# Attention rows normed one step later: inverses turned, moved and applied at later steps, three gate fills and one key projection moved with them

## The reference, cut to what matters

```python
a1 = _attn(q, k1, v1, causal=True)      # latent keys and a shared rotated key k_rope
a2 = _attn(q, ks, vs, causal=False)     # 32 selected tokens
a3 = _attn(q, kw, vw, causal=True)      # window keys
out = g[:, 0] * a1 + g[:, 1] * a2 + g[:, 2] * a3
return out.reshape(B, T, N_HEAD * V_HEAD) @ w_proj
```

## Time and profile before

| what | value |
|---|---|
| median of 3 runs | 1849.78 us (1848.2 to 1859.12) |
| the profiled execution, its own time | 1854.49 us |
| its span, first to last instruction | 1852.7 us |
| PE busy | 1715.3 us (93%) |
| ACT busy | 1220.4 us (66%) |
| DVE busy | 1158.5 us (63%) |
| POOL busy | 680.2 us (37%) |
| mean granted TensorE clock | 0.961 |

### The profile page before, as it was taken

One profiled execution on the slowest core, in us unless ns is written; L12 is line 12 of the kernel. 1 busy time (PEld: TensorE's weight loads), 2 busy tenths in 40 slices (PEclk: granted clock), 3 DMA queues, 4 the chain that ended last, 5 costly groups with the idle time before them and its releaser, 6 DMA issues.

```text
span 1852.7 us, 33815 instructions
## 1 busy us (share of the span) xinstructions
PE 1715.3 (93%) x10588; PEld 1067.9 (58%) x10588; DVE 1158.5 (63%) x3679; ACT 1220.4 (66%) x3383; POOL 680.2 (37%) x697
## 2 busy tenths in 40 slices
PE   5676689999999999999999999999999999999998
PEld 3433456665566656665666566665666566656664
DVE  5999666656555656655665656565565566565675
ACT  2564367766776757776676677675777677667773
POOL 0456533444333333434344433333333434443300
PEclk8787799999999999999999999999999999999999
DMA  4001021112111211212111211121122211121101
GB/s 171 1 0 28 17 64 41 41 37 64 27 43 36 51 44 41 52 45 52 41 41 36 64 29 43 38 50 42 41 52 45 52 41 41 40 62 30 42 19 46
DMA packets 71295, 80.91 MB, mean 44 GB/s; under 512 B 29520, under 2 KB 37840, under 8 KB 70992
## 3 DMA queue, kind: packets, MB, share of 16 engines
q1 hardware_dynamic: 71120, 78.76, 17.2%
HBM read 7.91 MB, written 2.10 MB: 5 GB/s over the span
## 4 chain that ended last, share of the span: by engine, by line
PE 72%; DVE 9%; ACT 8%; issue 6%; POOL 4%; DMA 0%; SPq 0%; DVEq 0%; POOLq 0%; ACTq 0%
PE bank L1862 24%; PE bank L1883 13%; PE bank L1826 8%; PE bank L1716 4%; PE bank L1717 3%; ACT arena L1002 2%; PE bank L1774 2%; PE bank L1789 2%; PE bank L1836 2%; DVE arena L1452 1%; PE bank L1712 1%; PE bank L1780 1%; PE bank L1783 1%; PE bank L1671 1%; PE bank L1770 1%
## 5 line engine op out<-in xcount | busy, mean ns | idle before, releaser
L1002 ACT ACTIVATE arena<-arena 128x512 f32<-128x512 f32 (+3 forms) x1024 | 571.4, 559 | 314.0 <-DVE arena L1452 309.2
L1452 DVE CUSTOM_DVE_ANT_0 arena<-bank,W 128x512 f32<-128x512 f32 (+3 forms) x1024 | 478.6, 487 | 464.9 <-PE bank L1862 436.7
L1862 PE MATMUL bank<-arena 96*128 96x512 f32 (+3 forms) x2048 | 698.8, 443 | 0.0
L1862 PEld LDWEIGHTS bank<-arena 96*128 96x128 f32 x2048 | 351.1, 192 | 192.6 <-issue 127.4
L1883 PE MATMUL bank<-W,arena 128*128 128x128 f32 x2560 | 420.1, 278 | 9.1 <-ACT arena L1002 7.1
L1883 PEld LDWEIGHTS bank<-W,arena 128*128 128x128 f32 x2560 | 309.6, 142 | 175.5 <-issue 103.7
L994 ACT ACTIVATE arena<-bank 128x512 f32<-128x512 f32 (+1 forms) x512 | 277.4, 542 | 126.4 <-PE bank L1883 121.6
L739 POOL TENSOR_TENSOR arena<-arena,one 128x512 f32<-128x512 f32 x64 | 66.5, 1040 | 722.3 <-DVE arena L1420 558.5
L1002 ACT ACTIVATION_READ_ACCUMULATOR arena<-arena 128x1 f32 x1024 | 195.9, 191 | 0.0
L1463 DVE COPY arena<-bank 128x384 f32<-128x384 f32 x256 | 141.8, 554 | 63.8 <-PE bank L1883 63.8
L1826 PE MATMUL bank<-arena 128*32 128x256 f32 (+1 forms) x3072 | 166.7, 350 | 0.0
(11 more groups left out here) (255 smaller groups left out, 2079.8 us busy)
## 6 DMA issues: line engine op xcount, KB each, us to landing
arena<-arena SPq DMA_DIRECT2D x896, 64.0 KB, 2.0
arena<-arena SPq DMA_DIRECT2D x64, 128.0 KB, 2.4
W<-wide SPq DMA_DIRECT2D x1, 3730.0 KB, 13.3
X<-x SPq DMA_DIRECT2D x8, 256.0 KB, 5.8
out<-arena SPq DMA_DIRECT2D x8, 256.0 KB, 2.3
arena<-arena SPq DMA_DIRECT2D x96, 16.0 KB, 1.8
LW<-lat SPq DMA_DIRECT2D x1, 768.5 KB, 14.3
arena<-mods SPq DMA_DIRECT2D x1, 768.0 KB, 4.7
```

The lines of the kernel that those rows point to most:

```text
L1002: done = A(here, here, ACT.Exp, bias=nmax[:, c:c + 1], scale=-1.0, accum_out=lsum[:, c:c + 1])
L1452: last = v.tensor_tensor_reduce(Pb[:, s % 4, at_p:at_p + n], bank[turn.score_bank(s)][:, at:at + n], w("mask", T - n), -1.0, 3e38, ALU.add ...
L1862: last = MM(B_[:, at:at + n], query(t), Kb[a][g % 2][0:QD, h, 0:n], start=True, stop=True)
```

## The change

In the second layer's attention, three of the five parts of a row are moved by one step: PE turns the inverses at step 15 of the row where it was 14, ACT copies them at 16 where it was 15, DVE norms at 17 where it was 16, and DVE adds the branches at 18 where it was 17. INVERT and the products with the values stay. In group 0 of a full turn `z4T`, `gf` and `gi` move by one step each, `gc` stays. In group 2 `kr` moves from 17 to 18, between the unmoved `cqkv` at 15 and `sel` at 19. The last turn gets one more trailing step, since its length is worked out from ADD. No instruction is added or taken away, and none changes its shape.

```diff
-INVERT, SPREAD, MOVE, NORM, ADD = 12, 14, 15, 16, 17
+INVERT, SPREAD, MOVE, NORM, ADD = 12, 15, 16, 17, 18
...
-        extra = [(7, "z3T"), (11, "score"), (12, "vs"), (13, "gates"), (21, "rank")] if first else [(13, "z4T"), (15, "gf"), (16, "gi"), (19, "gc")]
+        extra = [(7, "z3T"), (11, "score"), (12, "vs"), (13, "gates"), (21, "rank")] if first else [(14, "z4T"), (16, "gf"), (17, "gi"), (19, "gc")]
...
-        extra = [(15, "cqkv"), (17, "kr"), (19, "sel"), (21, "ks"), (22, "nqT")]
+        extra = [(15, "cqkv"), (18, "kr"), (19, "sel"), (21, "ks"), (22, "nqT")]
```

## The result

| what | before | after |
|---|---|---|
| median | 1848.99 us (4 runs) | 1888.42 us (4 runs, 1884.91 to 1889.67) |
| ratio, 95% interval | | 1.0206 [1.0187, 1.0225] |
| profiled execution, its span | 1854.49, 1852.7 us | 1889.22, 1887.4 us |
| mean granted TensorE clock | 0.961 | 0.955 |

The kernel became 39.4 us slower. The forecast was 1878, slower, with a range of 1850 to 1900: the sign and the range held, and the time is 10 us above the forecast.

A forecast was written before the change was run, and what follows sets the result against it. PE was taken to bound the kernel, busy 195 of 200 us per turn. Terms of 0.25 + 2.5 + 0.7 + 0.6 = 4.05 us per turn, seven turns, gave +28 on the 1849.78 median: 1878 us, range 1850 to 1900.

The forecast's parts named there:

- Part 2: Group 2, shared key: `sel` waits for ACT's reading of `kr` behind unit 18's exponential; +2.5 us per turn, bounds -0.6 to +2.9.
- Part 1: Group 0, `z4T`, spread, `gf`, `gi`: two waits go but others replace them; +0.25 us per turn, bounds -1.0 to +0.9.
- Part 3: Other rows: ACT's later copy delays readings and exponentials; +0.7 and +0.6 us per turn, bounds 0 to +3.8.
- The sum: All groups: 4.05 us per turn over seven turns, +28 us; 1882.5 on the profiled execution, 1878 on the median.
- the clock's term: TensorE clock falls behind PE's stops: the forecast left them unchanged and added nothing for them.
- a rival of +23 at 0.13: Group 2's 2.8 us stop brings the lower clock each turn, 3.3 us lost, seven times 23 us: 1901; chance 0.13.
- the forecast's own range: Whole kernel: 1862 (the key at its +1.9, nothing else) to 1890 us, for the forecast held at 0.55.
- nothing takes the place of the waits: Rival, faster: group 0's 2.5 us and group 2's 0.62 are gained, 3.1 per turn, 22 us: 1828; chance 0.10.
- the work is covered: Rival, within 1%: key costs 1 us or less, other rows nothing; 0 to 12 us, 1850 to 1862; chance 0.22.

The follow-up runs named there:

- The undoing: The changed kernel with the shared key's task `kr` back at step 17, all else as changed: 1862.08 us, ratio 1.0064 to the kernel before.
- the earlier reading: The changed kernel with ACT reading `kr` in step 18, ahead of the exponential of unit 18: 1866.37 us, ratio 1.0077 to the kernel before.
- the key alone: The kernel before with only `kr` moved from step 17 to 18: 1868.53 us, ratio 1.0105.
- the norming alone: The kernel before with DVE's norming and adding one step later (17, 18), spread and copy left at 14 and 15: 1851.20 us, ratio 0.9994.
- the copy late: The kernel before with ACT's copy, the norming and the adding one step later (16, 17, 18), PE's spread left at 14: 1860.13 us, ratio 1.0050.
- the turning alone: The kernel before with only PE's spread one step later (15), copy, norming and adding left in place: 1847.71 us, ratio 0.9985.
- the gates alone: The kernel before with only `z4T`, `gf` and `gi` of group 0 one step later: 1859.30 us, ratio 1.0049.

## Why the prediction was right, and where it was short

**Part 2 (the key, +2.5 per turn) held.** Set the replay beside the trace after by the start of ACT's reading of `cqkv` (767.79 in the replay, 979.59 in the trace, so 211.80 apart). Copy: replayed 771.03, so 982.83, measured 982.83. Norming: 771.7, so 983.50, measured 983.58. Maximum: 773.65, so 985.45, measured 985.54. Reading of `kr`: 775.15, so 986.95, measured 987.00. `sel`: 776.45, so 988.25, measured 988.23. One thing was left out: PE still turns probabilities from 985.40 to 985.89 (L1883), so its stop is 2.33 and not 2.8; the place of `sel` does not depend on it. And POOL's rotation of the key starts 2.66 later (988.25, against 773.79 before), not 3.9, which was a misreading that nothing hung on. From `cqkv` to `sel` the distance grew by 2.49 (978.40 to 988.23, against 7.34 before), and 0.18 more came behind `sel`. The undoing (A back to 12.09) and the earlier reading (no wait at `sel`) show the cause, and the key alone (+1.62) that the later rows add the rest.

**Part 1 (group 0, +0.25) held**, at +0.19. By the start of DVE's norming (861.63 and 873.03, 11.40 apart) the replay had the turning of unit 12 at 864.25, so 875.65, measured 875.65; `spread` behind 865.8, so 877.20, measured 877.23; the second values at 866.9, so 878.30, measured 878.32. Behind them `gi` waits 0.26 in the same turn (884.18), for ACT's reading of `gf`, where the replay had 0.4.

**Part 3 (the other rows, +1.3) held in size**, at 1.35 (C, D, G and H). That it comes from the copy's place was shown. Its split is only in part as replayed: in group 3 the wait for `nq` grew by 0.32 (+0.3 replayed), but the wait for the exponential by 0.55 (+0.35 replayed). Together that is more than C's +0.70, so some of it is made up in the rest of the stretch; what each term costs by itself was not measured.

**The sum** of the parts, 4.05 per turn, was measured as 4.21.

**The step that failed is the clock's term, taken as 0.** The prediction left the falls as they were, with a rival of +23 at 0.13 beside it. Between the medians the term measured about 10 us: the stretches make 29.5 of the 39.4, and 9.9 are left. That is nearly the whole of the miss (the three parts at 4.21 for 4.05 make 1.1 more); the direction and the three parts came out as worked out, and that 1888.42 still lies under the 1890 at the top of the forecast's own range is in part luck. Between the two profiled executions the falls can be placed. They cost 4.5 us more: +10.1 in group 2 (A and B), where the longer stop brought them in every turn, and -5.6 in group 0, where 0.7 was left of 6.3. So the rival was right that each turn would fall. It was too large, since four of seven turns fell there before, and it missed that another place would give back. To put the sum on the median was sound as long as the falls stayed as they were; 1882.5, the sum on the profiled execution, lies nearer to the result only because that execution happened to have more falls than a median one.

**The rivals.** That nothing takes the place of the waits fell: the total of the two stops in group 0 went from 2.48 to 2.43. That the work is covered fell too: group 2 alone cost 2.67 per turn. That by the rule of the Trainium skill, that idleness closes the clock, every turn would fall was the prediction's reading of it. Group 2 after agrees with the reading, with a fall in all seven turns; group 0 after does not, with its stop of 1.95 in every turn and a clock of 1.00 in five of the seven, and there the measurement decides. Nearer to this case is another section of that page of the Trainium skill, "TensorE: Matmul & The Clock Gate", Part 1 (A second HAM failure mode: psum-queue depth-cycling): in a kernel whose PE pauses often between groups of matmuls, the clock swings between its two levels, and the time is lost between the bursts. The windows of group 2, 0.66 to 0.92, are means of both levels and agree with the swinging. Where the time is lost they do not bear out: here the matmuls themselves run longer, `o2` behind `sel` for 1.75 us (L1783 at 990.32) where it took 1.13 before (776.33).

## What to carry to other kernels

A tile is free when the engine that reads it comes to that instruction in its list, not when the tile is done: before moving a task by one step, look at what stands ahead of its reading, and what that in turn waits for. Where several engines wait one after another behind one late event, moving the waiting instructions handed the stall here from one to the next; find the last name in the chain and move that one earlier, as one line of POOL's order did here for 22 us (1849.47 to 1827.19). And when a sum rests on one profiled execution, ask first how far that execution lies from the median, and in which stretches; what the clock adds or gives back is a term of its own.

## What the runs showed of the hardware that was not expected

The falls of the clock do not follow from the length of the stops alone. With the two stops of group 0 at 1.44 and 1.04 us, three turns of seven fell in the profiled execution of before (6.3 us in stretch E), two with the key alone, one with the norming alone and three with the copy late. With the turning alone moved, PE stood 1.44 and then 0.84 us in front of the values, and no turn fell; with the whole change 1.95 and 0.48, and two turns lost 0.7 in all. With one stop of 3.1 us (the gates alone) five turns of seven fell. In group 2 the two kernels with `kr` at 18 and read behind the exponential, the changed one and the key alone, lost 16.6 and 14.5 us to falls, and the other ten kernels between 5.2 and 11.1. So the longest stops, 3.1 in group 0 and 2.33 in group 2, went with the most falls of their place, but 1.95 went with almost none. One profiled execution of each kernel stands behind these counts. Why one turn falls and the next does not, after the same stops, stays open.
